# A transformer block on one core: masked maxima on VectorE, seven shared PSUM banks, and new orders of work

## The chip, the cores and the metric

The kernel runs on one core of a Trainium2 chip. The metric is the device time of one execution in microseconds; the time before is the median of three runs.

## The reference

Eight sequences of 1024 rows by 256 go through an attention layer with 16 heads of 16 (layer norm before it, rotary positions, causal mask, softmax, projection, layer norm of the result, residual) and through a feed-forward layer with low-rank weights (256 to 64 to 1024, GELU, 1024 to 64 to 256, again with norms and residual). All is float32.

```python
x = x + _layernorm(_L0_attn_ref(_layernorm(x), qkv_w, qkv_b, proj_w, proj_b))
x = x + _layernorm(_L0_ffn_ref(_layernorm(x), U1, V1, b1, U2, V2, b2))
# attention:
scores = jnp.einsum('bhid,bhjd->bhij', q, k) * scale
scores = jnp.where(causal, -jnp.inf, scores)
attn = jax.nn.softmax(scores, axis=-1)
out = jnp.einsum('bhij,bhjd->bhid', attn, v)
# feed-forward:
P = x @ U1
Q = jax.nn.gelu(P @ V1 + b1) @ U2
return Q @ V2 + b2
```

## The kernel before

Attention goes in 32 groups (8 batches, four groups of four heads each). Float32 queries and keys are split into two rounded parts, stored to HBM and loaded again so that one matmul over 48 rows adds the three products of parts (`load_group`, `QK`). For each group two passes over the scores follow. The first (`max`, L724) has queries on the partitions: in 12 steps (`MAXES`) it gives the largest score of each query. For steps with an open end, those that reach the diagonal, four more matmuls (L731) add a mask from `MASKQ` and `MASKK` into the bank; VectorE reduces the bank (`max_out`, L899). The maxima are turned by TensorE (`chain_turn`, L745), negated and split (`NSROW`), and sent as two more rows of `QK` (`shift`). The second pass (`score`, L762) has keys on the partitions and gives scores with the maximum subtracted, over 50 rows; ScalarE takes the exponential into `PB` (`exp`, L1077), GpSimd zeroes what is above the diagonal (`select`, L1155), and TensorE multiplies by the values and a column of ones into `PV` (`product`, L780), which ScalarE copies out (`ot_copy`, L1083).

A `max` or `score` step is cut into units by its width (`units`): up to 256 columns one unit has both pairs of heads, above that each pair has its own. So a group has 20 units of `max`, 12 of them with an open end, and 20 of `score`. A unit has two banks of PSUM, one for each head of the pairs. Six banks (`RING`) form three fixed couples, A, B and C; which one a unit takes is written in the order itself (capital letters for `max`, small ones for `score`). One bank (`MI`) serves all other steps in attention: transposes of x (`xt`), query and key blocks (`qk`, L688), `values` (L698), turns of maxima, and the projection (`proj`, L790, emptied by L923 and L924). The eighth bank is `PV`. TensorE may start a unit when its couple was emptied: `free` waits for the instruction that empties what stood there before (`AFTER`, `out_of`), which covers both heads at once.

The order on each engine is a written string of letters (`ORDERS`), one letter a step; `order_of_work` turns them into steps and banks. Every engine works off its string and waits for semaphores. While a group runs, the preparation of the next batch (`xt`, `qk`, rotation on GpSimd, `values`) and the projection of the last one are mixed in. The feed-forward layer follows with steps `up`, `down`, `gelu` and `f_y`, in the same PSUM banks.

Of the kernel before, what the change touches and what calls it, by code (L numbers as in the profile page):

```python
# [28 lines left out]
ROWS, SHIFT = 48, 50  # L29

# [83 lines left out]
def taken_by(engine, step):  # L114
# [4 lines left out]
    if what in ("f_norm", "f_res"):  # L119
# [8 lines left out]
    "PE": dict(x="xt", q="qk", v="values", f="fold", t="chain_turn", p="product", j="proj", T="f_turn",  # L128
# [15 lines left out]
        "xxqqxxqqqqvqvvvqfxxBAxBACxqqBqBFACBqABCBACBACABBAtCbACAbCqabCpqBcAqpaCBqAbppcBavCapCapabCvBCapcAbptabCAp"  # L144
        "cBApcBaCpbAcpBaCpaBcApBcpAbpcBaCaBcApbcApbaCpBtCapAbpcABpcACbapBcpAbCAbpCpaBcAbcpAbpCaBpaCbpABcpaBcptBca"
        "pCbApbCAbCpBapcAbCpaBcAbCpAbpcBaCpBapcAbpCbapCAbptbcApCbApCAbCbppabvCBvacBxpCaxABpcApbpqBcqABcqcBAcbqpCa"
        "bCptcBappcBaxCBapxCAjcBajpBpaqbCAqpCajABcjpbaCqBapqbpcpBavCaBvbaCpcBtpaBcpCBapaCBpCaBpCapbpAcpCabAcBpppA"
        "cBcapBaCbpaBcpBaCbpCtAbpbAcBAcpBCappbAcBaCpbApBcAcpBapcBacBApbcpAbCpacBBaptBapCbApCBapcpAbvCAbvCbxaCpBcp"
        "ACxabqabCpqAbCpqcaBqCBapcptCBappbaxCbpCaxBCApjacBjcBcqpAqBAcjBaCpjabpCqbpcApqpcAbvBcvBcApCbaptcBpcAbpaCB"
        "pABcAcpppbCapBcACbppbACbApcbpCaBpcAcBapbaCBCaptbaCpbACpAbCpaBpcAbCpaBcABcpAbcpAbpCaBpaCbpaCBpcAbptcBapAc"  # L150
        "BpCbApCbpavBCavaBCpapxcApCbaxCqcbAqaBCqabCpqcBApcBAppbcAtbpAbxCxAbCjpAbjaCpqcbApqCBajpACbjppbcAqbaCqcbAp"
        "vACpvabCpaBcptacBppCbACbpACbaBpApcBapBcpbCbaCpppBAcbCpBapCabBcapcBpACbtAbpCAbcpBCappbAcBCapABcpaAcBapcBp"
        "aCaBpabCpAbCpbaCtpcBaCbApCBpapCabvpaCBvCaxbCApBcpxAcbqAbcqApqpCbAqbaCcbpCpcAbptCaBpcAbxCxABcjpAjpCabqCbq"
        "bCApjBpcAjpbqAcppbapCqbcAvCbvaCpBcpBacbtApcBpAcBpCaBaCpbAppcBaCpAbcpBpaCbApcpbACpBacABcpacbpAtCpacBABcpA"
        "CbppaBcAbCpaBcAbCpAbcpBapCaBpcAbpAbCpbCaBtcapBcApBcApppbcAvABcvacBpaxBcAxpBcAqpcbAqcBApqcBaqbcpABpcbApCa"
        "tpBaxCBaxCAjpjcBapqBAcqpBaCjpBCajabpAcqbcpqAbCpvcABvpabCpCabptCabpAcBpaCBpcApcBAcpbCpBapaCbpaBpaBpaCpabC"
        "pAcbAcpBcApAcBtpCBaaCbpABcppaCbAbCpbApcBaCbApcBpaCBapCabpCaBcpacBtpAbCpBaCpbApCbapvBcAvcBapCbxaBpxaBCpqA"
        "bcqBaCqpbAcqaBCpAcbptpaCbpCxBaCxpabCjaBCjpbCqAcbqCpjbCApjpcaBqpBacqpACbvpAbvAcbApabCtpcAbpCBapCAbpCbpaBc"
        "ppABccApCbABcpappBcapBcAbCpbAcAbpcaBtpCBapcABcApbCaBpAcpbCaBpCAbpbCpabCapBCapbAcpbACpaCbpcAtbaCBpcApCbpp"
        "aCbvACbvBapCaBApjcaBjcAbpcpBcapcBpCaBpCaptCbAjcaBpCbApCBajCbappBaCpbApCbaBCapbApCbpaBcpAbCaBpcBapCtaBCap"  # L160
        "abCpAbCpbApcBCapABcpaCbApcbApcbApCAbpbCaCbptabcpbcpcbapppbaTbpbaTpbpapTbappabTpabUbapbapTuupppTduuTjuuTj"
        "uudUdduuTudduTddTuuTjUuujTuuyudduuTdTyuuTdddddUuyuuTddTuyuuTddduuTdddUdduuTuyuuddTuuyTuuTddddUdyuudTuudu"
        "yuTdddTuuTddUdduyuddTuuTyuudTuuTdUdduuyuddduyuuddddduydddduyddddyy",
    "ACT":
        "llllxxllqllqxxqqrqvqrqvvrqllllxrllxllvxxqqqFrqrteleqeelqeqeeqeeloveeeeveeeteeereeeeoeeeeeeeeoeeereeteeee"
# [12 lines left out]
        "ssssdssssdrrrsrlrsrrlwrrlssdsrfrsssrdlsmmssmsdsssmsdmmmXmmmmmmmmmmmmmmammmbmmmmmmmmmmmmmmmmmambmmmmmmmmm"
        "mmmmmmmmmambmmmmmmmmmmmmmmmmmmmmabmmmmmmmmmmmmmmmmmmmmambmmmmmmmimmmmmmmmmmmamibmmmmmmpmpSmSSSDmmmpmmpSS"
        "mSSDmmmmmambmmmmmmmmmmmmsmsmsmsmmdmmsammbsmmmmmmmmmmmmmmmmmmiambmsmmmmmmmmmmmmsdmimmmmmammbmmmmmpmpSSSmS"  # L180
        "DmmmpmmpSSSSDmmmmmmmabmmmmmmmmsmmmmmsssmmmmdmsmasmmsbsmmmmmmmmmmmmmmmmmmammbmmmmdmmmmmmmmmimmmmmimammbmm"
        "mpmmpSmSSSDmmmpmmpSSSSDmmmmmmmambmmmmmmmmmmmmmmmsssmsmdmammbmmmmmmmmmmmmsmmmmmmsassmdbmimmmmmmmmmmmmmimm"
        "mmmmambmmmmmpmpSSmSSDmmmpmpmmmSSSSDmmmmambmmmmmmmmmmssmsmsmmmmmdmmssssammbdmmmmmmmmmmmmmmmmmmmaimbmmmmmm"
        "mmmmimmmmmmmmmambmmmpmmpSSmSmSDmmmpmmpSSSSDmmmmmmmabmmmmmmmmmsmmsmmmssmmdmsmmsammbmmsmmmmmmmmmmmmmmsmmam"
        "bmmmmmmmmimmmmmdmmmimmmmambmmmmpmmpSmmSSmSDpmmpmSmSSmmmmmSaDmmbmmmmmmmmmmmmmmmmmmambmmmmmmmmmmmmmmmmmmmm"
        "aimbmmmmmmmmmmmpimpSSmmSSDmmmmabmmpmmmmmpmSmmmmmmmmSmmSmmSDmambmmmmmmmmmmmmmmmmmmabFWRFRFRFiURFpRFpSRUSi"
        "FRFSpSDRUpFRSSYYPSYYPFUYYSRPDYYFPURFYYRPYYPFURFYYPYRYFUPRYFYRYPYUPYYYPYPYYPYYPYYPYNYPANA",
    "POOL":
        "ppooppprrrrlrrlssssrrrrsrssssssslrlsssssssssssssssssssssspssrrarrassrlasasrPlssrsrrRsPlrRRRrsrslssssssps"
# [1069 lines left out]
```

## Time and profile before

| | before |
|---|---|
| median of 3 runs | 1340.21 us (1338.93 to 1342.71) |
| profiled execution, span | 1352.9 us |
| TensorE matmul busy | 1251.7 us, 11889 instructions |
| VectorE busy | 935.4 us, 1449 |
| ScalarE busy | 911.8 us, 1257 |
| GpSimd busy | 659.1 us, 724 |
| attention, with preparation of batches | to about 1150 us |
| feed-forward alone | from about 1150 us |

The profiled execution is a single one and 12.7 us longer than the median. The span is from its first to its last instruction; of its own time nothing besides the span is given. A matmul's row lasts until its results have left the array, so rows overlap, and busy time is the time in which at least one runs. The start of one step to the start of the next is a better measure of what a step costs TensorE.

### The profile page before, as it was taken

To read this page: it belongs to the slowest core of one execution; us is meant where nothing else is said; L and a number is where in the kernel's file an instruction comes from. 1 tells how busy PE (TensorE), PEld (TensorE's weight loads), DVE (VectorE), ACT (ScalarE), POOL (GpSimd) and SP (SyncE) were. 2 spreads that over 40 slices of the span, in tenths; PEclk is the share of its full clock that TensorE was granted. 3 is DMA by queue.
4 is the path that set the end of the run, shared out by engine and by line. 5 is a ranking of instruction groups with operands and counts; after the bars stand their busy time and mean duration, and the time that the engine had idled before them with its cause. 6 is when DMAs were issued, how large, how long until landed. Compare 5 with 4: busy or idle time off the path is not lost.

```text
span 1352.9 us, 29140 instructions
## 1 busy us (share of the span) xinstructions
PE 1251.7 (93%) x11889; PEld 618.4 (46%) x11889; DVE 935.4 (69%) x1449; ACT 911.8 (67%) x1257; POOL 659.1 (49%) x724
## 2 busy tenths in 40 slices
PE   6789999999999899989999999999999999999994
PEld 2344444544444444544444444444444554445452
DVE  4676776668766876667567767786776687666755
ACT  4326676677667667756767776777576668868784
POOL 4154412882288228812585249524842224426556
PEclk9669999999999999978999999999998899999997
DMA  6643563376626644645456455544474443501412
GB/s 198 162 105 60 119 90 60 84 167 90 119 84 136 109 62 129 127 97 90 70 125 155 68 103 135 149 79 89 117 137 76 80 84 104 159 19 63 156 56 101
DMA packets 99465, 142.43 MB, mean 105 GB/s; under 512 B 25222, under 2 KB 61188, under 8 KB 99332
## 3 DMA queue, kind: packets, MB, share of 16 engines
q1 hardware_dynamic: 99332, 140.58, 47.9%
q8 instruction: 93, 1.52, 0.5%
q14 instruction: 40, 0.33, 0.1%
HBM read 79.70 MB, written 51.38 MB: 97 GB/s over the span
## 4 chain that ended last, share of the span: by engine, by line
PE 73%; ACT 9%; DVE 6%; POOL 3%; DMA 3%; issue 3%; SPq 2%; ACTq 0%; POOLq 0%
PE PV L780 18%; PE RING L762 12%; PE RING L724 12%; PE MI L688 8%; ACT PB L1077 6%; PE MI L790 4%; PE RING L731 4%; PE MI L698 4%; PE RING L824 3%; PE RING L831 3%; DVE MB L899 3%; DVE M L899 2%; PE RING L803 1%; DMA head_sums<-OT 1%; PE MI L679 1%
## 5 line engine op out<-in xcount | busy, mean ns | idle before, releaser
L1077 ACT ACTIVATE PB<-RING 128x1024 f32<-128x1024 f32 (+2 forms) x640 | 582.9, 938 | 262.6 <-PE RING L762 245.4
L899 DVE TENSOR_REDUCE MB<-RING 128x2 f32<-128x1024 f32 (+2 forms) x448 | 502.1, 1145 | 190.7 <-PE RING L724 95.6
L1155 POOL TENSOR_SCALAR_AFFINE_SELECT PB<-PB 128x512 f32<-128x512 f32 x256 | 161.6, 637 | 431.9 <-ACT PB L1077 431.6
L724 PE MATMUL RING<-QK 48*128 48x512 f32 (+3 forms) x1536 | 286.6, 406 | 33.3 <-ACT PB L1077 15.9
L762 PE MATMUL RING<-QK 50*128 50x512 f32 (+3 forms) x1536 | 278.0, 406 | 23.0 <-ACT PB L1077 12.0
L899 DVE TENSOR_REDUCE M<-RING 128x2 f32<-128x768 f32 (+1 forms) x186 | 190.6, 1044 | 89.1 <-PE RING L731 88.2
L780 PE MATMUL PV<-PB,VL 128*32 128x512 f32 (+3 forms) x2048 | 234.8, 536 | 2.2 <-ACT OT L1083 1.4
L724 PEld LDWEIGHTS RING<-QK 48*128 48x128 f32 x1536 | 142.3, 193 | 199.9 <-ACT PB L1077 87.5
L762 PEld LDWEIGHTS RING<-QK 50*128 50x128 f32 x1536 | 134.7, 190 | 185.7 <-ACT PB L1077 72.7
L731 PEld LDWEIGHTS RING<-MASKK,MASKQ 64*128 64x128 f32 x1536 | 144.2, 199 | 8.1
L731 PE MATMUL RING<-MASKK,MASKQ 64*128 64x64 f32 (+1 forms) x1536 | 130.8, 249 | 0.0
L688 PE MATMUL MI<-XT,WQ 128*32 128x512 f32 x912 | 114.6, 622 | 1.8 <-ACT EO L1040 1.0
L780 PE MATMUL PV<-PB,VU 128*32 128x512 f32 (+3 forms) x1024 | 94.9, 455 | 0.8 <-POOL PB L1155 0.7
L1102 ACT ACTIVATE F_H<-RING,F_B 128x512 f32<-128x512 f32 x128 | 80.3, 687 | 21.6 <-PE RING L824 21.5
L469 POOL TENSOR_TENSOR TA<-EO,COS 128x1024 f32<-128x1024 f32 x28 | 66.6, 2377 | 44.5 <-ACT EO L1040 44.0
L480 POOL TENSOR_TENSOR EO<-EO,PARTS 128x1024 f32<-128x1024 f32 x28 | 66.5, 2375 | 21.9 <-ACT PARTS L1045 21.9
L780 PEld LDWEIGHTS PV<-PB,VL 128*32 128x32 f32 x2048 | 43.7, 109 | 62.6 <-issue 44.4
L1040 ACT ACTIVATE EO<-MI,BQS 128x512 f32<-128x512 f32 x57 | 39.1, 687 | 46.2 <-PE MI L688 46.0
L471 POOL TENSOR_TENSOR TB<-EO,SIN 128x1024 f32<-128x1024 f32 x28 | 66.6, 2378 | 0.0
L790 PE MATMUL MI<-WP,ATT 128*32 128x256 f32 x1024 | 61.8, 381 | 0.4 <-POOL ATT L1160 0.3
L831 PE MATMUL RING<-F_H,F_U 128*64 128x512 f32 x256 | 61.1, 604 | 0.0
L698 PE MATMUL MI<-WQ,XT 128*32 128x256 f32 x928 | 56.0, 382 | 0.1
(121 smaller groups left out, 1257.7 us busy)
## 6 DMA issues: line engine op xcount, KB each, us to landing
QK<-split_parts SPq DMA_DIRECT2D x372, 128.0 KB, 5.9
split_parts<-PARTS SPq DMA_DIRECT2D x60, 256.0 KB, 3.1
split_parts<-EO SPq DMA_DIRECT2D x60, 256.0 KB, 3.4
ATT<-OT SPq DMA_DIRECT2D x128, 64.0 KB
INV<-inverse_sums SPq DMA_DIRECT2D x32, 256.0 KB
block_mid<-Y SPq DMA_DIRECT2D x16, 512.0 KB, 3.6
F_X<-block_mid SPq DMA_DIRECT2D x16, 512.0 KB, 5.2
out<-F_Y SPq DMA_DIRECT2D x32, 256.0 KB, 2.1
```

Source lines behind the costliest of these rows:

```text
L688: ins = e.matmul(bank[r:r + 32, :], WQ[:, k, 128 * m + r:128 * m + r + 32], XT[:, k, 512 * c:512 * c + 512], start=(k == 0), stop=(k == 1))
L698: ins = e.matmul(m[r:r + 32, 256 * (j - j0):256 * (j - j0) + 256], XT[:, k, 128 * j + r:128 * j + r + 32], WQ[:, k, 512:768], start=(k == ...
L724: ins = e.matmul(m[:, h, i, :], QK[g % 3][r, 0, k, 128 * t:128 * t + 128], QK[g % 3][r, 1, k, k0:k0 + n], start=(i == 0), stop=not open_en ...
L731: ins = e.matmul(m[:, h, :, n - 128 + 64 * z:n - 64 + 64 * z], MASKQ[r, z, :], MASKK[r, z, :].unsqueeze(1).to_broadcast([64, len(pairs), 64]),
L762: ins = e.matmul(m[:, h, i, :], QK[g % 3][r, 1, k, 128 * j:128 * j + 128], QK[g % 3][r, 0, k, 512 * c + off:512 * c + 512], start=True, st ...
L780: ins = e.matmul(PV[32 * h:32 * h + 32, off:512], v[:, n0:n0 + 32], PB[(SLOTS * g + s) % 4][:, h, 0:n], start=(j == 0), stop=(j == 4 * c + 3))
L790: ins = e.matmul(m[r:r + 32, 256 * (q - q0):256 * (q - q0) + 256], ATT[c][:, k, 128 * q + r:128 * q + r + 32], WP[:, k, :], start=(k == 0) ...
L831: ins = e.matmul(QP[64 * a:64 * a + 64, :], U2[:, f, :], H[i % 2][:, a, f, :], start=(f == 0), stop=(f == 7))
L899: e.tensor_reduce(acc, ring(("max", g, s, u), pairs, n), AX.X, ALU.max).then_inc(v_max, 1)
L1077: e.activation(buf[:, :, pairs[0]:pairs[-1] + 1, :], ring(("score", g, s, u), pairs, n), ACT.Exp).then_inc(a_exp, 1)
L1102: e.activation(H[i % 2][:, a, f, :], GP[(NTH["up", i, f] - 1) % 2][a], ACT.Gelu_apprx_tanh, bias=B1[:, f:f + 1]).then_inc(f_g, 1)
L1155: e.affine_select(buf[:, :, 0:128], buf[:, :, 0:128], pattern=[[0, 4], [1, 128]], base=0, channel_multiplier=-1, compare_op=ALU.is_ge, fil ...
```

## The change

The mask matmuls are removed. A table `TRI` (zeros, and in its last 128 columns the mask) is loaded once, and VectorE takes maxima of units with an open end by an instruction that adds the table to the scores, writes the sums back into the bank and gives the maximum, one for each head and each pair. Other maxima and all exponentials are split into one instruction for each of the two heads of a unit (`by_head`; both thresholds are zero), and each frees its own bank (`counts_by_head`). `RING` has seven banks; each step, the former `MI` steps among them, takes any of them by a string of digits (`BANKS_TAKEN`), a unit any two. The bias addition of the projection is one instruction. The orders of all engines are new, and for batches 1 to 6 they repeat.

```diff
+SPLIT_MAX, SPLIT_EXP = 0, 0
...
+FEED = {("f_turn", 0, 0): (5, 6), ("up", 0, 0): (1, 2), ("up", 0, 1): (3, 4), ("f_y", 0, 0): (0,)}
...
+        order[engine] = [next(left[LETTERS[engine][letter]]) for letter in letters]
+    digits = iter(BANKS_TAKEN)
     for step in order["PE"]:
+        if step in FEED:
+            bank[step] = FEED[step]
+        elif step[0] in EMPTIES.values():
+            bank[step] = tuple(int(next(digits)) for _ in range(2 if step[0] in ("max", "score") else 1))
+        else:
+            continue
+        after[step] = list(dict.fromkeys(had[i] for i in bank[step] if i in had))
+        had.update((i, (step, h)) for h, i in enumerate(bank[step]))
     return order, bank, after
+
+def by_head(step):
+
+    what, g, s, u = step
+    if what == "max_out":
+        return open_end(g, s) or reach(g, s)[3] > SPLIT_MAX
+    return width(s)[3] > SPLIT_EXP
+
+def counts_by_head(steps, what):
+
+    found, n = {}, 0
+    for step in steps:
+        if step[0] == what:
+            parts = 2 if by_head(step) else 1
+            for h in range(2):
+                found[step[1:] + (h,)] = n + min(h + 1, parts)
+            n += parts
+    return found
...
-            MASKQ = sb("MASKQ", [128, 2, 128], fp32r)
-            MASKK = sb("MASKK", [128, 2, 64], fp32r)
+            TRI = sb("TRI", [128, 512])
...
-        RING = ctx.enter_context(nc.psum_tensor("RING", [128, 6, 512], fp32))
+        RING = ctx.enter_context(nc.psum_tensor("RING", [128, 7, 512], fp32))
...
+            e.dma_start(TRI[:, :], tri).then_inc(s_mask, 16)
...
                 elif what == "f_fill":
+                    w.wait_ge(g_res, max(NTH["residual", NB - 2, c, 2] for c in range(2)))
                     load_f(1)
...
-                                           QK[g % 3][r, 1, k, k0:k0 + n], start=(i == 0), stop=not open_end(g, s))
-                    if open_end(g, s):
-                        w.wait_ge(v_mask, 1)
-                        for z in range(2):
-                            for h in range(2):
-                                r = slice(64 * h, 64 * h + 64)
-                                ins = e.matmul(m[:, h, :, n - 128 + 64 * z:n - 64 + 64 * z], MASKQ[r, z, :],
-                                               MASKK[r, z, :].unsqueeze(1).to_broadcast([64, len(pairs), 64]),
-                                               start=False, stop=(z == 1))
+                                           QK[g % 3][r, 1, k, k0:k0 + n], start=True, stop=True)
...
-                    e.tensor_reduce(acc, ring(("max", g, s, u), pairs, n), AX.X, ALU.max).then_inc(v_max, 1)
+                    found = ring(("max", g, s, u), pairs, n)
+                    if open_end(g, s):
+
+                        w.wait_ge(s_mask, 16)
+                        for h in range(2):
+                            for i in range(len(pairs)):
+                                scores = found[:, h, i, :]
+                                ins = e.tensor_tensor_reduce(out=scores, in0=scores, in1=TRI[:, 512 - n:512], scale=1.0, scalar=-3.0e38,
+                                                             op0=ALU.add, op1=ALU.max, accum_out=acc[:, h, i].unsqueeze(1))
+                            ins.then_inc(v_max, 1)
+                    else:
+                        for heads in (slice(0, 1), slice(1, 2)) if by_head(step) else (slice(0, 2),):
+                            e.tensor_reduce(acc[:, heads], found[:, heads], AX.X, ALU.max).then_inc(v_max, 1)
...
-                    e.tensor_tensor(YS[c][:, q0, :], MI[:, 0:256], BP[:, :], ALU.add)
-                    e.tensor_tensor(YS[c][:, q0 + 1, :], MI[:, 256:512], BP[:, :], ALU.add).then_inc(o_mi["proj"], 1)
+                    e.tensor_tensor(YS[c][:, q0:q0 + 2, :], BANKS[BANK["proj", b, c, q0][0]].rearrange("p (q d) -> p q d", q=2),
+                                    BP[:, :].unsqueeze(1).to_broadcast([128, 2, D]), ALU.add).then_inc(o_mi["proj"], 1)
...
-                    e.activation(buf[:, :, pairs[0]:pairs[-1] + 1, :], ring(("score", g, s, u), pairs, n), ACT.Exp).then_inc(a_exp, 1)
+                    scores = ring(("score", g, s, u), pairs, n)
+                    for heads in (slice(0, 1), slice(1, 2)) if by_head(step) else (slice(0, 2),):
+                        e.activation(buf[:, heads, pairs[0]:pairs[-1] + 1, :], scores[:, heads, :, :], ACT.Exp).then_inc(a_exp, 1)
```

The part of the diff that is left out holds the new strings, the removed loads of the mask's pieces and their waits, and the replacement of `MI` by the bank that a step has.

## Rows read from the trace of the kernel before

**Rows 1.** The page: busy time, share of the span, instructions by engine.

```profile
PE 1251.7 (93%) x11889; PEld 618.4 (46%) x11889; DVE 935.4 (69%) x1449; ACT 911.8 (67%) x1257; POOL 659.1 (49%) x724
```

**Rows 2.** The chain of work that ended last: shares of the span by line.

```profile
by line: PE PV L780 18.1%; PE RING L762 12.2%; PE RING L724 11.9%; PE MI L688 7.5%; ACT PB L1077 5.6%; PE MI L790 4.0%; PE RING L731 3.7%; PE MI L698 3.6%; PE RING L824 3.4%; PE RING L831 3.3%; issue 2.9%; DVE MB L899 2.8%; DVE M L899 1.9%;
```

**Rows 3.** Stretches of four groups: length, busy (instructions), clock, DMA; sum of all four.

```profile
core 0: us, PE busy (x) PEld busy (x) DVE busy (x) ACT busy (x) POOL busy (x), PEclk, DMA share, GB/s
288.00:429.00 141.00, 132.76 (x1379) 64.99 (x1375) 99.74 (x131) 98.26 (x130) 77.69 (x79) 1.00 0.55 110
...
854.00:987.00 133.00, 128.75 (x1356) 64.21 (x1352) 97.89 (x129) 95.22 (x124) 70.95 (x71) 1.00 0.54 107
sum 546.00, PE 521.36 PEld 259.18 DVE 393.51 ACT 386.02 POOL 296.36; mean PE 130.34 PEld 64.80 DVE 98.38 ACT 96.50 POOL 74.09
```

**Rows 4.** TensorE in order of time, 826 to 838: start, length, what.

```profile
826.11 0.73 PE L724 MATMUL RING<-QK 48*128 48x512 f32 x4
826.68 0.33 PE L762 MATMUL RING<-QK 50*128 50x384 f32 x2
826.99 1.92 PE L688 MATMUL MI<-XT,WQ 128*32 128x512 f32 x16
828.73 0.61 PE L780 MATMUL PV<-PB,VU 128*32 128x256 f32 x8
...
833.50 0.34 PE L731 MATMUL RING<-MASKK,MASKQ 64*128 64x128 f32 x4
833.68 0.45 PE L762 MATMUL RING<-QK 50*128 50x256 f32 x4
...
836.58 1.06 PE L780 MATMUL PV<-PB,VL 128*32 128x512 f32 x8
837.57 0.50 PE L724 MATMUL RING<-QK 48*128 48x512 f32 x2
```

**Rows 5.** TensorE in order of time, two more masks and what follows them.

```profile
721.06 0.31 PE L731 MATMUL RING<-MASKK,MASKQ 64*128 64x64 f32 x4
721.30 1.07 PE L780 MATMUL PV<-PB,VL 128*32 128x512 f32 x8
...
722.58 0.31 PE L731 MATMUL RING<-MASKK,MASKQ 64*128 64x64 f32 x4
722.72 0.42 PE L762 MATMUL RING<-QK 50*128 50x128 f32 x4
```

**Rows 6.** The page: the mask matmuls as a group, busy us and mean ns.

```profile
L731 PE MATMUL RING<-MASKK,MASKQ 64*128 64x64 f32 (+1 forms) x1536 | 130.8, 249 | 0.0
```

**Rows 7.** Groups by shape, VectorE, 288 to 566: busy us, mean ns.

```profile
L899 DVE TENSOR_REDUCE MB<-RING 128x2 f32<-128x1024 f32 x80 | 96.1, 1222 | 38.6 <-PE RING L724 25.9 <-PE RING L731 12.4
...
L899 DVE TENSOR_REDUCE M<-RING 128x4 f32<-128x512 f32 x8 | 5.5, 690 | 5.9 <-PE RING L731 5.8
```

**Rows 8.** VectorE and ScalarE in order of time: instructions without a wait between.

```profile
820.70 2.35 DVE L899 TENSOR_REDUCE M<-RING 128x2 f32<-128x1024 f32 x2
...
823.25 1.94 ACT L1077 ACTIVATE PB<-RING 128x1024 f32<-128x1024 f32 x2 [0.23 <-PE RING L762]
...
838.29 0.38 DVE L935 BATCH_NORM_AGGREGATE YMV<-YST 128x2 f32<-128x6 f32 x4
```

**Rows 9.** Groups by shape, whole span: an addition from PSUM and SBUF.

```profile
L923 DVE TENSOR_TENSOR Y<-MI,BP 128x256 f32<-128x256 f32 x32 | 13.6, 424 | 28.2 <-PE MI L790 27.7
```

**Rows 10.** Groups by shape, ScalarE, 288 to 566: the exponentials.

```profile
L1077 ACT ACTIVATE PB<-RING 128x1024 f32<-128x1024 f32 x114 | 113.6, 1023 | 47.4 <-PE RING L762 45.1 <-PE PV L780 1.5
...
L1077 ACT ACTIVATE PB<-RING 128x512 f32<-128x512 f32 x16 | 9.5, 596 | 9.2 <-PE RING L762 6.5 <-PE PV L780 2.7
```

**Rows 11.** A stretch of the feed-forward stage, columns as in rows 3.

```profile
1150.00:1250.00 100.00, 99.74 (x752) 48.44 (x746) 62.79 (x203) 80.10 (x133) 44.03 (x66) 1.00 0.26 82
```

**Rows 12.** Two stretches with a fallen clock, columns as in rows 3.

```profile
566.00:719.00 153.00, 143.43 (x1369) 70.09 (x1368) 99.01 (x130) 98.62 (x130) 74.88 (x77) 0.91 0.49 103
...
599.00:605.00 6.00, 6.00 (x35) 3.19 (x37) 3.74 (x6) 1.57 (x4) 0.63 (x1) 0.50 0.00 0
```

**Rows 13.** TensorE in order of time: the wait ahead of that fall.

```profile
593.59 0.63 PE L724 MATMUL RING<-QK 48*128 48x128 f32 x4 [1.80 <-ACT PB L1077]
```

More of the change, by code:

```diff
@@ L127 @@
 LETTERS = {
-    "PE": dict(x="xt", q="qk", v="values", f="fold", t="chain_turn", p="product", j="proj", T="f_turn",
+    "PE": dict(m="max", s="score", x="xt", q="qk", v="values", f="fold", t="chain_turn", p="product", j="proj", T="f_turn",
                U="f_u1", u="up", d="down", y="f_y", F="first_turn"),
@@ L149 @@
[L149 to L153, printed above, removed]
@@ L243, in block_kernel @@
     ORDER, BANK, AFTER = order_of_work()
+    MAXED, EXPED = counts_by_head(ORDER["DVE"], "max_out"), counts_by_head(ORDER["ACT"], "exp")
     NTH = {}
@@ L371, in block_kernel @@
         s_spread = sem("s_spread")
-        v_half, v_one, v_pv0, v_bvw, v_mask = (sem(f"v_{n}") for n in ("half", "row", "pv_zero", "bias_wide", "mask"))
+        v_half, v_pv0, v_bvw = (sem(f"v_{n}") for n in ("half", "pv_zero", "bias_wide"))
         a_cst = sem("a_consts")
@@ L450, in ring, with last_of @@
         def ring(step, pairs, n):
-            first = BANK[step][0] - 1
-            return RING[:, first:first + 2, 0:len(pairs) * n].rearrange("p h (k n) -> p h k n", n=n)
-        SCORED = [sum(len(units(width(i)[3])) for i in range(s + 1)) for s in range(SLOTS)]
+            i, j = BANK[step]
+            return RING[:, i:j + 1:j - i, 0:len(pairs) * n].rearrange("p h (k n) -> p h k n", n=n)
+        def last_of(g, s, n):
+            return g, s, len(units(n)) - 1, 1
         SELECTS = [sum(diagonal(i) for i in range(s + 1)) for s in range(SLOTS)]
@@ L518, in sync @@
             e.dma_start(BP[:, :], b_proj.partition_broadcast(128)).then_inc(s_wp, 16)
-            w.wait_ge(v_one, 1)
-            for h in range(2):
-                e.dma_start(stage[64 * h + 63:64 * h + 64, 128:256], ROW[0:1, :]).then_inc(s_mask, 16)
             e.dma_start(X[1][:, :, :], x_rows[1]).then_inc(s_x[1], 16)
@@ L665, in free @@
                 for before in AFTER[step]:
-                    w.wait_ge(*out_of(before))
+                    w.wait_ge(*out_of(*before))
             def bank_of(step):
@@ L768, in tensor @@
                     b = g // 4
-                    w.wait_ge(a_exp, UNITS * g + SCORED[s])
+                    w.wait_ge(a_exp, EXPED[last_of(g, s, width(s)[3])])
                     if diagonal(s):
@@ L796, in tensor @@
                     w.wait_ge(f_xh, n + 1)
-                    if (n, k) == (0, 0):
+                    if step in FEED:
                         free(step)
@@ L815, in tensor @@
                     w.wait_ge(f_lo, i + 1)
-                    w.wait_ge(a_exp, UNITS * NG)
+                    w.wait_ge(a_exp, EXPED[last_of(NG - 1, SLOTS - 1, width(SLOTS - 1)[3])])
                     w.wait_ge(f_g, 2 * (NTH[step] - 2))
+                    if step in FEED:
+                        free(step)
                     m, cols = GP[(NTH[step] - 1) % 2], slice(128 * f, 128 * f + 128)
@@ L840, in tensor @@
                     w.wait_ge(f_y, 2 * (NTH[step] - 1))
+                    if step in FEED:
+                        free(step)
                     for j in range(2):
```

188 lines of the change are left out of this document (95 added, 93 removed).

## The prediction

> **What bounds the kernel now.** I read the page first, then tables of stretches, then instructions grouped by shape, then single stretches of TensorE in order of time. The page [rows 1] gives TensorE 93% of the span, VectorE 69% and ScalarE 67%; but a busy matmul row includes the emptying of its pipeline, so 93% doesn't yet say how much TensorE could be relieved. The chain of waits [rows 2] runs mostly over TensorE (3.7% of the span, 50 us, on the mask matmuls L731), and 10.3% (139 us) over the three lines that empty score banks: exponentials L1077 and maxima L899. So two things set the pace: what TensorE has to issue, and how soon a bank is free again.
>
> The table of stretches [rows 3] takes four times four groups of heads, about 1364 matmuls each; the first and the last stretch are shown. They last 141 to 133 us, 546 us for 16 groups, 34.1 us a group, all at full clock. In them VectorE is busy 98.4 us on average, 24.6 us a group, ScalarE 24.1 and GpSimd 18.5.
>
> For what TensorE must issue I take the distance from the start of one step to the start of the next where no idle time stands between them [rows 4, 5]. A product of 512 columns: 836.58 to 837.57, 0.99 us; those of 384, 256 and 128 columns I put at 0.78, 0.55 and 0.33, a little over their share. Two units of 512 columns: 826.11 to 826.68, so 0.285 each; one unit of 384 columns 0.31. The 16 matmuls of a query/key block: 826.99 to 828.73, 1.74 us; values and projection have the same columns in 32 matmuls, for which I take 1.85. A group has 6 products of 512 and two of each other width (9.3 us), 24 units of 512 columns (about 0.31 with their hand-over, 7.5), 8 of 384 (2.4), 4 of 256 and 4 of 128 (some 0.34 and 0.26, 2.4), and a quarter of a batch's 16 blocks of 1.8 us, 4 transposes of x and 4 turns of maxima (8.2). The mask: 721.06 to 721.30, 722.58 to 722.72 and 833.50 to 833.68, so 0.24, 0.14 and 0.18 us, mean 0.19, 12 times a group [rows 4 to 6]: 2.3 us. Sum 32.1 us. Of the 34.1 us some 2.0 are stalls, in which TensorE waits for a bank: that is what the chain's 139 us stand for, where they exceed the issue.
>
> **Part by part.** *The mask matmuls go.* 1536 of them over 32 groups are 130.8 us busy, but by start distances 12 x 0.19 = 2.3 us a group, 32 x 2.3 = 74 us. The bounds are the chain's 50 us [rows 2] and the 131 us of busy time [rows 6]. I take 74, which is measured as distance on the engine that sets the pace. What is late next is the emptying. Every open unit also gets to VectorE by these 0.2 us sooner.
>
> *VectorE adds the mask.* 12 reductions a group become 32 instructions that add, take the maximum and write the sums back into the bank. The columns are the same, 4 x 1280 x 2 = 10240 a group. The trace has reductions of 1024 and 512 columns at 1222 and 690 ns [rows 7]: 1.04 ns a column and 160 fixed. Two back to back last 2.35 us, not 2.44 [rows 8], so an added instruction costs 160 - 90 = some 0.07 to 0.08 us. An addition from PSUM and SBUF of 256 columns takes 424 ns [rows 9], the same 1.04 a column and 157 fixed, so a second input costs nothing more. The maximum that is carried out besides is not in this trace. Its lower bound is nothing; the nearest row above is the smallest VectorE instruction, four in 0.38 us [rows 8], 0.095 each. So 20 added instructions cost 1.5 us a group, and the carrying out 0 to 3.0 us more. The writing back into PSUM is not in the trace either; nearest is the same addition with its output in SBUF, so I take nothing, and for the other end one more pass over the columns, which is the slow rival below. I take 1.5 us for the carrying out, the middle, as no row stands nearer to one end.
>
> The Trainium skill (VectorE: DVE Perf Modes, Two Vector instructions with no wait between them) says that an instruction which also writes out its accumulator counts as two, the second of them an accumulator read. By that rule the upper end of 3.0 us would hold, and VectorE would be busy 29.7 us a group, not 28.2; no row of before shows such an instruction. The same page (the errata section) advises tiles of 512 elements or more because each instruction pays a fixed cost; that speaks against a 128-column unit in four pieces, and the 160 ns above agree.
>
> *Maxima of the 8 closed units head by head.* 8 more instructions of 0.075 us, 0.6 us a group. VectorE: 24.6 + 1.5 + 1.5 + 0.6 = 28.2 us a group (26.7 to 29.7). It is hidden as long as TensorE needs more; that cover is 29.8 us, thin at the upper end. The projection's bias addition becomes one instruction from two: 0.3 us a batch, nothing.
>
> *Exponentials head by head.* An exponential of 1024 elements takes 1023 ns, of 512 elements 596 [rows 10], so 170 ns fixed; two without a wait last 1.94 us, not 2.05 [rows 8], so a split costs 0.07 us back to back and 0.17 with no overlap. The second head has no wait of its own, so I take 0.075: 20 x 0.075 = 1.5 us, ScalarE 25.6 us a group (27.5 at the other end). Hidden under TensorE.
>
> *Seven banks, any two for a unit.* TensorE's issue is the same. Today a unit of 1024 elements holds both banks for filling 0.6, some 0.2 of pipeline, mask 0.2 and emptying 1.2, or 2.2 us; 40 units hold 88 pair-microseconds of the 3 x 34.1 = 102. Then the first head's bank is free 0.6 us sooner and there is no mask: about 1.8 on average per bank, 40 x 2 x 1.8 = 144, with some 15 for the steps that had bank 0 to themselves, of 7 x 31.7 = 222. From 86% filled to 72%: this works on the 2.0 us of stalls. Against it stands that VectorE and ScalarE are nearer to full and that a block of queries or keys may now wait for a maximum. I let both cancel and keep the stalls' share, 6% of the group: 29.8 / 0.94 = 31.7 us a group.
>
> *Orders.* The letters are the same steps; in the stages after attention [rows 11] TensorE is busy 99.7 of 100 us and nothing of its work changes, so I leave them at zero, plus or minus 8 us. At the start 12 small loads and two copies for the mask go and one load of the table comes, nothing on the path, and the new order may gain or lose 8 us there. The added wait of the second weights' fill on SP is for a residual that the load ahead of it had waited for already: nothing is queued longer.
>
> **Sum.** The profiled execution has 1352.9 us; (34.1 - 31.7) x 32 = 77 us come off, to 1276. The median is 12.7 us below that execution's span, so 1263 us.
>
> **The rivals.** *Stalls nearly vanish* (seven banks and half-unit releases do more than the added VectorE work takes): 30.0 us a group, 4.1 x 32 = 131 off, 1209 us. For: the chain has 139 us on emptying [rows 2]. Against: VectorE at 28.2 of 30.0.
>
> *VectorE takes the place of the banks*: with 29.7 us of its own and a fixed order, it needs the same 6 to 10% of slack that TensorE has, 29.7 / 0.89 = 33.4 us a group, 22 us off, 1318 us. It decides where VectorE's own need passes TensorE's 29.8 us, with a carrying out of about 0.1 us.
>
> *Slower: the masked maximum needs a pass more per column* (write back and maximum at half the rate). 10240 x 1.04 = 10.6 us a group, VectorE 37.3 us a group at least, 3.2 x 32 = 102 us more than now, 1442 us. It decides where VectorE passes 34.1 us a group, 5.9 us more than the 28.2, or 32 masked maxima 0.18 us longer each than I put them: one of 512 columns above 0.9 us. Against: every PSUM row of VectorE so far has 1.04 ns a column.
>
> *The clock.* After 1.80 us in which TensorE waited for an exponential, the granted clock went from 1.00 to 0.50 (2.4 to 1.2 GHz), and the four groups with that stretch took 153 us, not 137 [rows 3, 12, 13]. With TensorE less full such gaps may come in every batch: 7 more at 16 us are 112 us, 1375 us. It decides from five more falls. For: VectorE and ScalarE nearer to the pace make longer gaps. Against: TensorE stays at 94%. *That the change doesn't do what it says*: with VectorE and TensorE in each other's way the group stays at 34.1 us, 1340 us.
>
> The Trainium skill (SBUF, Who interferes with whom) says that a VectorE instruction with at most one SBUF input doesn't contend with GpSimd. The masked maximum reads one input from PSUM and one from SBUF, so this page gives no loss for GpSimd's rotations; no row of before shows the new form beside them.
>
> **How the numbers follow.** Forecast, 1225 to 1300 us: 0.55. Vanishing stalls, 1190 to 1225: 0.12. VectorE crowded, 1300 to 1336: 0.15. No change, within 0.3% of 1340 (about what a measurement of this kernel can tell): 0.05. A pass more: 0.05. The clock: 0.08. Faster 0.82, same 0.05, slower 0.13. The range leaves out the two slow cases and a part of the fastest: 1205 to 1336 us.
>
> **What would show it.** TensorE with 1536 fewer matmuls and about 1.8 to 2.4 us a group less by start distances; VectorE busy 1003 to 1098 us in all (935.4 + 32 x 2.1 to 5.1), ScalarE 960 (up to 1021); a masked maximum of 512 columns at 0.69 to 0.79 us; a batch in 127 us; waits of weight loads for banks not longer than now. A batch over 134 us, a masked maximum over 0.9 us, or a granted clock under 0.93 would show it wrong, as would orders that change the start or the end by over 15 us.

## The result, and the profile after

| | before | after |
|---|---|---|
| median, four runs each on one chip | 1341.46 us (1338.93 to 1351.63) | 1294.64 us (1286.58 to 1296.05) |
| ratio, 95% interval | | 0.9605 (0.9535 to 0.9674) |
| profiled execution, span | 1352.9 us | 1292.8 us |
| TensorE busy | 1251.7 us | 1196.3 us |
| VectorE busy | 935.4 us | 1022.4 us |
| ScalarE busy | 911.8 us | 943.9 us |

The kernel is 4% faster: 47 us by the medians, 60 us by the two profiled spans. The forecast was 77 us. Ratios here and below are to the kernel before on the same chip and leave out executions over 1.5% above the fastest of their kernel, while medians hold all of them. First the page of the changed kernel, busy time by engine and below it the chain that ended last, by engine (as [rows 1]):

```profile
PE 1196.3 (93%) x10353; PEld 518.1 (40%) x10353; DVE 1022.4 (79%) x3333; ACT 943.9 (73%) x1897; POOL 658.5 (51%) x724
...
PE 51%; DVE 22%; DMA 9%; SPq 8%; ACT 4%; POOL 3%; issue 3%; ACTq 0%; POOLq 0%; DVEq 0%
```

TensorE has exactly the 1536 mask matmuls less (11889 - 10353). What is new is the chain: VectorE has 22% of it, and DMA and SP's queue 17%. Before, the page gave VectorE 6% of the chain, and DMA and SP's queue 5%.

The first five batches that have the same order (batch by batch from turn to turn; columns as in [rows 3]):

```profile
270.50:407.40 136.90, 129.91 (x1173) 55.00 (x1173) 109.59 (x366) 101.34 (x210) 74.79 (x76) 0.95 0.55 111
407.40:535.30 127.90, 124.83 (x1172) 53.34 (x1172) 109.56 (x366) 101.17 (x210) 74.83 (x77) 0.99 0.56 119
535.30:670.60 135.30, 127.76 (x1172) 54.58 (x1172) 109.44 (x366) 101.36 (x209) 74.77 (x77) 0.96 0.57 112
...
800.90:937.20 136.30, 129.46 (x1173) 54.62 (x1173) 109.48 (x366) 101.39 (x210) 74.88 (x77) 0.95 0.55 112
sum 666.70, PE 637.66 PEld 270.80 DVE 547.57 ACT 506.51 POOL 374.09; mean PE 127.53 PEld 54.16 DVE 109.51 ACT 101.30 POOL 74.82
```

The work is the same in each, but three last 135 to 137 us at a granted clock of 0.95 or 0.96, and two, the fourth among them, 128 and 130 us. These 20 groups take 33.33 us each; the same 20 took 34.97 us before (699.3 us, with one fall of the clock in them, of 27 us). So 32.6 of the 60.1 us of span come from this stretch, 17.8 from the six groups ahead of it (199.9 to 182.1 us), 12.3 from the five after it (156.1 to 143.8), and nothing from the start (88.2 and 88.4 us to the first turn) or the end (209.4 and 211.8 us after the last).

VectorE's instructions of the maxima by shape over the whole span: busy us, mean ns, idle before (as [rows 7]):

```profile
L936 DVE TENSOR_REDUCE MB<-RING 128x1 f32<-128x512 f32 x512 | 317.1, 680 | 64.4 <-PE RING L759 62.9
L931 DVE CUSTOM_DVE_ANT_0 RING<-RING,TRI 128x512 f32<-128x512 f32 x256 | 171.8, 719 | 21.6 <-PE RING L759 19.8
...
L931 DVE DVE_READ_ACCUMULATOR2_ANT MB<- 128x1 f32 x512 | 71.8, 140 | 0.0
...
L931 DVE CUSTOM_DVE_ANT_0 RING<-RING,TRI 128x128 f32<-128x128 f32 x256 | 66.7, 326 | 15.3 <-PE RING L759 15.3
```

A masked maximum is two instructions in the trace: one that adds and reduces, 719 ns for 512 columns and 326 for 128, and an accumulator read of 140 ns. By the columns that is 1.02 ns each and 195 ns fixed, so no second pass over the columns. The Trainium skill (VectorE: DVE Perf Modes, Two Vector instructions with no wait between them) says that an instruction with an accumulator output counts as two; the trace agrees, with the read's 140 ns as its own row.

### The profile page after: what moved, and what is told of

It reads as the page before. It is cut to its first block, busy times and chain, and to the rows that moved or that the text cites. A ratio compares the mean times of both kernels' runs of the same rounds, so it can differ in the third digit from the quotient of the medians.

```text
span 1292.8 us, 29708 instructions
## 1 busy us (share of the span) xinstructions
PE 1196.3 (93%) x10353; PEld 518.1 (40%) x10353; DVE 1022.4 (79%) x3333; ACT 943.9 (73%) x1897; POOL 658.5 (51%) x724
## 4 chain that ended last, share of the span: by engine, by line
PE 51%; DVE 22%; DMA 9%; SPq 8%; ACT 4%; POOL 3%; issue 3%; ACTq 0%; POOLq 0%; DVEq 0%
PE PV L807 12%; DVE RING L931 10%; PE RING L759 8%; PE RING L789 8%; PE RING L723 7%; DMA head_sums<-OT 6%; DVE MB L936 5%; PE RING L817 4%; SPq L597 4%; PE RING L860 3%; PE RING L733 3%; PE RING L853 3%; DMA X<-x 2%; ACT PB L1117 2%; SPq L628 1%
## 5 line engine op out<-in xcount | busy, mean ns | idle before, releaser
L1117 ACT ACTIVATE PB<-RING 128x512 f32<-128x512 f32 (+2 forms) x1280 | 618.0, 565 | 152.1 <-PE RING L789 146.4
L931 DVE CUSTOM_DVE_ANT_0 RING<-RING,TRI 128x128 f32<-128x128 f32 (+3 forms) x1024 | 469.5, 522 | 58.9 <-PE RING L759 55.4
L936 DVE TENSOR_REDUCE MB<-RING 128x1 f32<-128x512 f32 x512 | 317.1, 680 | 64.4 <-PE RING L759 62.9
L807 PE MATMUL PV<-PB,VL 128*32 128x512 f32 (+3 forms) x2048 | 245.9, 553 | 5.3 <-ACT OT L1123 4.3
L723 PE MATMUL RING<-XT,WQ 128*32 128x512 f32 x1024 | 124.0, 614 | 2.2 <-ACT XT L1072 1.4
L1142 ACT ACTIVATE F_H<-RING,F_B 128x512 f32<-128x512 f32 x128 | 78.1, 691 | 10.7 <-PE RING L853 9.2
L1078 ACT ACTIVATE EO<-RING,BQS 128x512 f32<-128x512 f32 x60 | 41.6, 694 | 43.5 <-PE RING L723 31.7
L931 DVE DVE_READ_ACCUMULATOR2_ANT MB<- 128x1 f32 x512 | 71.8, 140 | 0.0
L931 DVE DVE_READ_ACCUMULATOR2_ANT M<- 128x1 f32 x496 | 69.3, 140 | 0.0
L817 PE MATMUL RING<-WP,ATT 128*32 128x256 f32 x1024 | 64.4, 394 | 1.9 <-DVE Y L961 1.0
L733 PE MATMUL RING<-WQ,XT 128*32 128x256 f32 x1024 | 61.7, 388 | 0.0
```

Source lines behind the costliest of these rows:

```text
L723: ins = e.matmul(bank[r:r + 32, :], WQ[:, k, 128 * m + r:128 * m + r + 32], XT[:, k, 512 * c:512 * c + 512], start=(k == 0), stop=(k == 1))
L733: ins = e.matmul(m[r:r + 32, 256 * (j - j0):256 * (j - j0) + 256], XT[:, k, 128 * j + r:128 * j + r + 32], WQ[:, k, 512:768], start=(k == ...
L807: ins = e.matmul(PV[32 * h:32 * h + 32, off:512], v[:, n0:n0 + 32], PB[(SLOTS * g + s) % 4][:, h, 0:n], start=(j == 0), stop=(j == 4 * c + 3))
L817: ins = e.matmul(m[r:r + 32, 256 * (q - q0):256 * (q - q0) + 256], ATT[c][:, k, 128 * q + r:128 * q + r + 32], WP[:, k, :], start=(k == 0) ...
L931: ins = e.tensor_tensor_reduce(out=scores, in0=scores, in1=TRI[:, 512 - n:512], scale=1.0, scalar=-3.0e38, op0=ALU.add, op1=ALU.max, accum ...
L936: e.tensor_reduce(acc[:, heads], found[:, heads], AX.X, ALU.max).then_inc(v_max, 1)
```

## The experiments

The experiments ran on several chips, on which the kernel before had medians of 1344 to 1352 us. So they are compared by their ratios; 1% is 13 us. A difference of two ratios has an interval of about plus or minus 1% (13 us), with e6, e7 or e9 in it 1.4% (19 us), unless another is given.

### Where do the long batches come from?

Around 612 us of the changed kernel. VectorE, TensorE and SP's queue in order of time; in brackets the idle time before a row and what ended it:

```profile
611.64 0.68 DVE L936 TENSOR_REDUCE MB<-RING 128x1 f32<-128x512 f32 x1
617.47 0.55 DVE L955 RECIPROCAL SUM<-SUM 128x64 f32<-128x64 f32 x1 [5.16 <-DMA SUM<-head_sums]
617.95 0.63 DVE L936 TENSOR_REDUCE MB<-RING 128x1 f32<-128x512 f32 x1
```

```profile
618.72 0.79 PE L759 MATMUL RING<-QK 48*128 48x256 f32 x4 [3.86 <-DVE MB L936]
```

```profile
598.13 5.68 SPq L597 DMA_DIRECT2D QK<-split_parts  x12
603.85 2.43 SPq L628 DMA_DIRECT2D ATT<-OT  x2
606.32 1.07 SPq L631 DMA_DIRECT2D head_sums<-OT  x2
615.71 0.38 SPq L635 DMA_DIRECT2D SUM<-head_sums  x1
```

The reciprocal of the softmax sums (`att_inverse`, letter `i`) waits 5.16 us for its transfer. The maxima queued behind it had their scores long before, the last by 612.8: TensorE stands still for 3.86 us, waiting for a bank that VectorE would have freed. The sums are late because SP issues twelve loads of queries and keys first, then the stores of attention output and sums, and can issue the load of the sums only once their stores have landed, 9.4 us after it began to issue them. What TensorE's clock does then (stretches of the same trace, columns as in [rows 3]; the clock stands behind POOL's busy time):

```profile
612.00:618.00 6.00, 2.86 (x28) 1.05 (x24) 0.84 (x3) 3.11 (x6) 5.92 (x5) 1.00 0.23 38
618.00:624.00 6.00, 5.28 (x25) 2.50 (x26) 3.94 (x13) 1.49 (x4) 2.42 (x2) 0.55 0.29 88
624.00:630.00 6.00, 6.00 (x49) 2.61 (x49) 2.75 (x7) 2.66 (x5) 4.73 (x3) 0.60 0.20 54
```

After the gap the clock is at its lower level, 1.2 GHz, for most of 12 us, although TensorE has work in nearly all of them. A batch with such an event lasts 5 to 9 us longer than the others. Gaps of this length stand at four places of the trace (3.44 us at 221, 3.51 at 355, 3.86 at 618, 3.34 at 886). **e4** moves the reciprocal behind five more maxima in the orders of batches 1 to 6 and changes nothing else:

```diff
-...mamibmmmmmmmmmmmimmmmmpmmmapb...
+...mamibmmmmmmmmmmmmmmmmipmmmapb...
```

> The changed kernel, with one edit: in batches 1 to 6 VectorE's second reciprocal of the row sums comes five maxima later in its order. In four of the batches the trace shows VectorE idle for 4.6 to 5.2 us in front of it, waiting for a load of sums, then TensorE idle for 3.3 to 3.9 us, and then a granted clock of 0.5. Theory A (this wait costs some 8 us in each of four batches, stall and clock): 25 to 32 us less, about 1265 us, ratio to the changed kernel 0.975 to 0.98. Theory B (TensorE is held by its own work and the gap only moves to where the projection waits for the sums): under 5 us.

Measured: 1267.08 us (1263.41 to 1276.96), ratio 0.9393 (0.9322 to 0.9464), 2.1% of the time before, 27 or 28 us, below the changed kernel. Two of its batches (columns as before):

```profile
269.10:395.60 126.50, 123.47 (x1172) 52.85 (x1172) 109.30 (x366) 101.10 (x209) 74.83 (x77) 1.00 0.55 120
395.60:522.10 126.50, 123.49 (x1172) 52.88 (x1172) 109.31 (x366) 101.13 (x209) 74.75 (x77) 1.00 0.57 120
```

Each of these batches lasts 126.5 us, 31.6 us a group, and the clock doesn't fall in the five that have the same order. The idle time of VectorE ahead of its 16 reciprocals, whole span, in the kernel before, after, and e4, one row of each:

```profile
L917 DVE RECIPROCAL SUM<-SUM 128x64 f32<-128x64 f32 x16 | 8.7, 544 | 4.9 <-DMA SUM<-head_sums 4.9
```

```profile
L955 DVE RECIPROCAL SUM<-SUM 128x64 f32<-128x64 f32 x16 | 8.8, 549 | 21.1 <-DMA SUM<-head_sums 21.1
```

```profile
L909 DVE RECIPROCAL SUM<-SUM 128x64 f32<-128x64 f32 x16 | 8.8, 548 | 0.0
```

So the new orders brought this wait from 4.9 to 21.1 us, and it cost 27 us of the time. It is the orders and not the table: e3 below, with the old orders, the table and seven banks, waits 4.7 us there.

**e8** tries the other end: SP issues the stores of attention output and sums (`a`) ahead of the twelve loads (`g`).

```diff
-...hbgamob...
+...hbagmob...
```

> The changed kernel, with one edit on SP: in batches 1 to 6 the loads and sums of the batch's last product half are issued ahead of the next group's twelve loads, not behind them. In the changed kernel the sums' transfer starts at 606.9 us, behind 5.7 us of issues, and lands 8.8 us later, and VectorE waits for it. Theory A (the wait comes from the place in the queue and from the loads' traffic): VectorE's wait in front of the second reciprocal goes, and the time falls as in the run with the reciprocal later, by 20 to 30 us, unless the twelve loads, now some 6 us later, are missed. Theory B (the transfer itself is what lasts): the wait stays over 3 us and the time within 8 us of the changed kernel.

Measured: 1317.32 us, 0.9761 (0.97 to 0.9822), some 21 us slower than the changed kernel. SP's queue in e8:

```profile
615.50 1.07 SPq L585 DMA_DIRECT2D head_sums<-OT  x2
616.61 5.52 SPq L551 DMA_DIRECT2D QK<-split_parts  x12
622.17 0.42 SPq L589 DMA_DIRECT2D SUM<-head_sums  x1
```

and its reciprocals, and one of them in order of time:

```profile
L909 DVE RECIPROCAL SUM<-SUM 128x64 f32<-128x64 f32 x16 | 8.8, 548 | 31.7 <-DMA SUM<-head_sums 31.7
```

```profile
630.75 0.55 DVE L909 RECIPROCAL SUM<-SUM 128x64 f32<-128x64 f32 x1 [5.56 <-DMA SUM<-head_sums]
```

The stores are early now, but the load that brings the sums back is issued behind the twelve loads, and the reciprocal starts 8.6 us after its issue: the wait grew to 31.7 us. In both orders the leg of the round trip that is issued behind the twelve loads takes 8 to 9 us. **e10** is e4 and e8 together:

> Both edits together, the reciprocal five maxima later and the sums ahead of the loads. Theory A (the one stall has two cures): no better than the run with the later reciprocal, 1267 us, within 5. Theory B (the sums also hold the projection back): 5 to 15 us less.

Measured: 1265.28 us, 0.9387 (0.9326 to 0.9449), the same as e4. Once nothing is queued behind the wait, its place on SP doesn't matter.

### What were the masks worth?

**e1** is the kernel before without the mask matmuls. It leaves out the mask in the maxima (the maximum is then taken over keys that are not allowed, too), so its time is that of the same work less the masks. Orders and banks are those of before.

```diff
-                    if open_end(g, s):
-                        w.wait_ge(v_mask, 1)
-                        for z in range(2):
-                            ...
```

> The kernel before, with its orders and its three couples of banks, but without the mask matmuls (L731); the maxima are then taken over unmasked scores, so the mask of the maxima is left out and the softmax's shift is larger than needed. It isolates what TensorE gains from being rid of them. Theory A (the prediction's term, by distances from mask to next step): 2.3 us a group, 74 us or more, so about 1267 us or ratio 0.945. Theory B (score steps hand over faster to a mask than to other steps, so part of the mask's distance comes back as a longer hand-over): 1.5 us a group, 48 us, about 1293 us, ratio 0.964. Theory C (the mask lay beside waits for banks): under 25 us, ratio above 0.98.

Measured: 1315.98 us against 1352.34 on the same chip, 0.9724 (0.9644 to 0.9805), 36 us. I had put 74. TensorE in order of time, in the kernel before (rows that [rows 5] left out) and in e1, at the same steps of the same order:

```profile
720.88 0.34 PE L724 MATMUL RING<-QK 48*128 48x384 f32 x2
...
722.30 0.44 PE L724 MATMUL RING<-QK 48*128 48x384 f32 x2
...
722.97 0.45 PE L724 MATMUL RING<-QK 48*128 48x512 f32 x2
...
723.50 1.07 PE L780 MATMUL PV<-PB,VU 128*32 128x512 f32 x8
```

```profile
692.27 0.34 PE L724 MATMUL RING<-QK 48*128 48x384 f32 x2
692.54 1.06 PE L772 MATMUL PV<-PB,VL 128*32 128x512 f32 x8
693.54 0.44 PE L724 MATMUL RING<-QK 48*128 48x384 f32 x2
693.82 0.34 PE L754 MATMUL RING<-QK 50*128 50x128 f32 x4
693.99 0.45 PE L724 MATMUL RING<-QK 48*128 48x512 f32 x2
694.37 1.07 PE L772 MATMUL PV<-PB,VU 128*32 128x512 f32 x8
```

From a maximum's start to the step behind its mask, 720.88 to 721.30, 722.30 to 722.72 and 722.97 to 723.50, are 0.42, 0.42 and 0.53 us. Without the mask, 692.27 to 692.54, 693.54 to 693.82 and 693.99 to 694.37, they are 0.27, 0.28 and 0.38. So these masks cost 0.15, 0.14 and 0.15 us, where from the mask's start to the next row there are 0.24, 0.14 and 0.24. A part of that distance stays when the mask goes: the first maximum took 0.18 us to the mask (720.88 to 721.06) and takes 0.27 to the product. At 298 of the 384 masked units neither trace has idle time or the lower clock; compared in this way they give 0.14 us a mask on average, 1.7 us a group, 53 us in all.

The other part of the miss is what TensorE does with the time. The same 20 groups, before and in e1 (columns as in [rows 3]):

```profile
288.00:987.30 699.30, 665.09 (x6826) 329.57 (x6822) 492.52 (x650) 484.94 (x637) 371.54 (x376) 0.98 0.53 108
```

```profile
284.80:963.10 678.30, 632.46 (x5862) 267.08 (x5860) 491.03 (x650) 482.97 (x637) 370.46 (x376) 0.97 0.54 111
```

TensorE is busy 1.63 us a group less, but its idle time rises from 1.71 to 2.29 us a group, so that 1.05 us a group are left, 34 us. Over the whole span it waits 27.9 us for maxima instead of 19.9, 31.7 for exponentials instead of 27.9, and 6.3 for the loads of the turned maxima instead of 1.1.

**e5** and **e6** ask the same with the new orders and banks: e5 takes plain maxima by head and no mask (that part of the computation is left out), e6 is e5 with the mask matmuls on TensorE again.

```diff
-                    if open_end(g, s):
-                        ...
-                                ins = e.tensor_tensor_reduce(out=scores, in0=scores, in1=TRI[:, 512 - n:512], ...)
-                    else:
-                        for heads in ...
+                    for heads in (slice(0, 1), slice(1, 2)) if by_head(step) else (slice(0, 2),):
+                        e.tensor_reduce(acc[:, heads], found[:, heads], AX.X, ALU.max).then_inc(v_max, 1)
```

> The changed kernel, but units with an open end are reduced plainly, one instruction for each head, without adding the table (the mask of the maxima is left out, neither TensorE nor VectorE does it). It takes away the 32 table additions with their accumulator reads and puts 24 reductions a group there. VectorE should need 26.2 us a group or less instead of 27.4. Theory A (VectorE's added work is hidden under TensorE): within 8 us of the changed kernel. Theory B (VectorE is in the pace with TensorE): 20 to 50 us less.

> The changed kernel with its new orders and seven banks, but the mask is again added by TensorE in four matmuls a unit, and VectorE reduces plainly head by head. Against the run without any mask it prices the mask matmuls in the new orders; against the changed kernel it undoes the move from TensorE to VectorE alone. Theory A (2.3 us a group of TensorE's path): 74 us more than without a mask. Theory B (1.5 us a group): 48 us more. If VectorE's addition costs nothing on the path, it stands as much above the changed kernel.

Measured: e5 1279.49 us, 0.9497 (0.9424 to 0.957); e6 1317.55 us (1298.31 to 1323.84), 0.9697 (0.9575 to 0.9819). On TensorE the mask costs 2.0% here, 27 us, give or take 19; on VectorE, after against e5, 1.1%, 15 us. So the move itself brings about 0.9%, 12 us, which is not clear of nothing: the intervals of e6 and of the changed kernel overlap. **e12**, e5 with e4's order (mask left out as well), has 1260.44 us, 0.9351 (0.9269 to 0.9434):

> The run with the later reciprocal, and no table added by VectorE nor mask by TensorE (the mask of the maxima is left out). Without the later reciprocal the same removal was worth 15 us. Theory A (VectorE's table work costs only because it made the stall in front of the reciprocal longer; otherwise it lies under TensorE): within 6 us of the run with the later reciprocal. Theory B (it is in the pace everywhere): 12 to 20 us less.

Against e4 that is 0.4%, give or take 1.1%. With the wait for the sums gone, no cost of the 61 us of added VectorE work (1.9 us a group) is seen, but the 15 us that it costs in the changed kernel are not excluded either.

### Banks, halves and orders

**e2** is the changed kernel with the orders of before and their three fixed couples, **e3** the same with any of seven banks, so the masked maxima and the halves are in both. **e9** is e2 with an instruction for a whole unit again, where it has up to 512 elements a head and no mask is added.

In e2 and e3 `ORDERS` is that of before with the letters A to C read as `m` and a to c as `s`. The start of `BANKS_TAKEN` in e2 (couples, and bank 0 for the steps that had `MI`) and in e3 (the bank that was least recently taken):

```diff
-BANKS_TAKEN = "012345601253601400034120341256000340340125634012345634125634...
+BANKS_TAKEN = "012345601234560123456123045612304561230451623045162304152603...
```

And e9 against e2:

```diff
-SPLIT_MAX, SPLIT_EXP = 0, 0
+SPLIT_MAX, SPLIT_EXP = 512, 512
```

> The changed kernel's code (mask added by VectorE, head by head, own release of each bank), but with the orders and the fixed couples of banks of the kernel before. It leaves out of the change its new orders and the free choice of banks. Theory A (the gain is that of TensorE's masks, orders and banks give little): ratio to before 0.96 to 0.97, as the change. Theory B (the old orders don't suit VectorE's added 2.8 us a group, banks and orders bring the gain): 0.985 to 1.01. TensorE's distances a group should fall by the same 1.5 us in either.

> As the run with old orders and couples, but every step takes any of seven banks (the one used longest ago of those that are free without a deadlock). What it gains on that run is the worth of seven banks with the same orders. Theory A (banks relieve the stalls of some 2 us a group): 30 to 60 us less than with couples. Theory B (stalls come from fixed orders and from waits for DMAs, not from banks): under 15 us.

> The changed kernel's code with the old orders and couples of banks, and with exponentials and closed maxima in one instruction for both heads; only the table additions are apart. Against the run with old orders and couples it prices the split with its early release where banks are three couples. Theory A (the split's 0.075 us a unit is more than paid back by the early release): 10 to 30 us more than with the split. Theory B (nothing on the path): within 8 us.

Measured: e2 1412.47 us, 1.0419 (1.0318 to 1.052); e3 1356.1 us, 1.0027 (0.9982 to 1.0071); e9 1376.16 us, 1.0198 (1.0099 to 1.0297). In fixed couples halves alone lose: e9 is 2.2%, some 30 us, faster than e2, which neither expectation had. That a couple is free only with its second half, while the split costs instructions, is how I read it; no run tells it by itself. The seven banks give 3.9%, 53 us, back (e2 to e3), and the new orders with the banks that they take 4.2%, 57 us, more (e3 to the changed kernel).

**e7** leaves orders, banks and instructions, and only lets both banks of a unit come free with its second half; **e11** does so for the exponentials alone.

```diff
-                found[step[1:] + (h,)] = n + min(h + 1, parts)
+                found[step[1:] + (h,)] = n + parts
```

> The changed kernel, but both banks of a unit are released only after the second head's instruction. The instructions are the same; only the early release of the first bank is undone. Theory A (banks are in the pace): 20 to 50 us more. Theory B (the early release by about 0.6 us lies beside TensorE's other work): under 8 us more.

> The changed kernel, but only units of scores release both banks after the second exponential; maxima release theirs one by one. Undoing both cost 93 us. Theory A (TensorE's weight loads waited for ScalarE's emptying 148 us in all and for VectorE's some 125 us, so both sides share): 35 to 60 us more than the changed kernel. Theory B (VectorE, the fuller engine, is the side that matters): under 25 us more.

Measured: e7 1387.63 us, 1.0205 (1.0084 to 1.0326), 6.0% of the time before above the changed kernel; e11 1306.29 us, 0.97 (0.9626 to 0.9775), 1.0% above it, at the edge of the noise. The waits of TensorE by what ended them (us in total, times, longest), first in the changed kernel, then in e7:

```profile
PE RING L789 <- DVE M L931: 4.2, 18, 0.2
...
PE RING L789 <- DVE MB L931: 3.0, 13, 0.4
PE RING L759 <- DVE M L931: 2.0, 6, 0.6
PE RING L759 <- DVE MB L931: 1.5, 5, 0.5
```

```profile
PE RING L789 <- DVE MB L931: 22.5, 48, 1.0
...
PE RING L789 <- DVE M L931: 12.5, 25, 1.0
...
PE RING L759 <- DVE MB L931: 9.8, 18, 0.8
PE RING L759 <- DVE M L931: 7.7, 18, 1.1
```

In these rows TensorE waits 52.5 us for masked maxima instead of 10.7, and its clock falls more often (23 falls and 143 us at the lower level from 120 us to the end of attention, against 10 and 61; the trace of e7 is of an execution of 1391.26 us). The bank of the first head, free 0.6 us sooner, is worth about 80 us here, most of it on VectorE's side. This is an upper bound: the orders were made for the early release. The reverse, whole units in the new orders, was not tried.

## Why the prediction was right, and where it was not

**Direction.** TensorE's issue and the freeing of banks set the pace, and the kernel gained on both (e1, e3, e7), as forecast. The time, 1294.64 us, lies in the range, 32 us above the 1263. One of my own signs spoke against the forecast: a batch over 134 us. Three of the five batches last 135 to 137.

**Profiled span and median.** 14.5 of these 32 us are in the last step of the sum. I took off 12.7 us, by which the profiled span of before lay above its median; the span of after lies 1.8 us below its own. A gain worked out as a difference of spans should have been taken as it is, or the offset should have widened the range. The span itself was forecast at 1276 and is 1292.8.

**The mask matmuls, 74 us.** Mis-sized, in two steps. A mask takes TensorE 0.14 to 0.15 us and not 0.19, because I read the start distance behind the mask as the mask's own cost, while a part of it belongs to the neighbours: 53 us in all, near the chain's 50 [rows 2]. And of the 1.63 us a group that TensorE is busy less in e1, 0.58 come back as waits. That leaves 36 us in the old orders (e1); in the new ones it is 27, give or take 19 (e6 against e5). I had called the chain's 50 us the lower bound, and the worth lies below it.

**The masked maxima.** VectorE is at 27.4 us a group (28.2 forecast, 26.7 to 29.7) and 1022 us in all (1003 to 1098). In parts I had both sizes off, in opposite directions: splitting added 20 instructions for 0.9 us (e5 25.5, before 24.6), 0.045 each and not 0.075; table and accumulator reads added 1.9 us (after 27.4), 0.06 for each of 32, where I took 0.047. One of 512 columns in e4 takes 0.65 us from its start to the next row's (606.68 to 607.33), under the 0.69 to 0.79 forecast. The rows (719 ns) exclude the pass more per column. The upper end of 3.0 us, two instructions by the Trainium skill's rule (VectorE: DVE Perf Modes, Two Vector instructions with no wait between them) with 0.095 us as the price of the second, was too many, though the count of two is what the trace has. I had the added work as hidden; the table and its reads cost 15 us as the kernel is (e5), and nothing that is seen once the wait for the sums is gone (e12).

**Exponentials by head.** 25.3 us a group for 25.6 forecast, 944 us for 960. That they are hidden was not tested by themselves; together with the split maxima they cost 30 us in fixed couples (e2 against e9).

**Seven banks and fuller engines cancel.** The net was close, but zero was the wrong way to say it. Fixed couples with halves and table are 4.2% slower than before (e2), seven banks take 3.9% off again (e3), and early release carries 6% in the new orders (e7). Terms of 53 to 80 us stood on either side of my zero.

**Orders at zero.** Right for start and end (0.2 and 2.4 us), wrong for attention, where I had given them nothing: the new orders with their banks are worth some 57 us (e3 to after). With the mask matmuls left on TensorE, orders, banks and halves already reach 0.9697 (e6); by the middle values three quarters of the gain is theirs. The one that I took for the largest, the mask's move, brings some 12 us there, which the intervals don't tell from nothing.

**The stalls.** I kept them at 6% and came to 31.7 us a group. e4 has 31.6: the rate that I forecast is that of the changed kernel without its wait for the sums. As two terms of the sum were wrong in opposite directions (the masks too large, the orders at zero), this agreement is partly luck. The kernel itself has 33.3, and what I missed is one letter in VectorE's order with a DMA behind it. The orders stood in the change, SP's queue in the trace of before, and I costed both at nothing.

**The rivals.** *The clock* came in part: ten falls instead of two from 120 us to the end of attention, 61 us at the lower level instead of 48. Seven of the ten lie in the five batches with the same order, where e4 has none though only the reciprocal's place differs; so they came with VectorE's wait for a DMA and not with a wait for exponentials. e4 has four falls in all in attention, 24 us. *VectorE crowded* gave 33.4 us a group, near the 33.3 measured, but by another mechanism: e4 runs at 31.6 us a group with VectorE just as full (109.3 us of 126.5). *Stalls vanish* and *no change* didn't come.

## What to carry to other kernels

A wait for a DMA in the order of an engine that frees buffers is paid by whoever needs the buffers: put it where the transfer, and all that its queue issues before it, is surely through. Price a small instruction by comparing the same steps with and without it, not by the distance to the next row, since a part of that distance belongs to the neighbours, and expect a part of what it frees to come back as waits. When a change holds several parts whose effects you let cancel, their size belongs in the range: here banks, orders and early release were each larger than the net gain of 47 us.

## What was not expected of the hardware

- An accumulator read of 140 ns overlaps its neighbours: only about 60 ns of it show as occupancy (1.9 us a group for 32 reads, 8 instructions more among them).
- The sums, 4 KB a store, took 9.4 us from the issue of the stores to the issue of the load behind them in the changed kernel (606.32 to 615.71), and 8.6 us from the issue of the load, of 32 KB, to the reciprocal in e8 (622.17 to 630.75). In both cases twelve loads of 128 KB had been issued ahead of that leg, in the changed kernel with two stores of attention output between.
- A maximum of 384 columns ahead of a product takes TensorE 0.27 us behind a score step (e1, 692.27 to 692.54), and ahead of a score step behind a product 0.28 (693.54 to 693.82). With a mask of four small matmuls between, both take 0.42: 0.14 to 0.15 more, though the masks' own rows last 0.31.
